# A decoder on one core: in cross-attention, ScalarE's PSUM copy is put ahead of both exponentials of the next step, and its other copies between them

## What is computed

```python
Q = _proj(input_Q, Wq, bq)   # (B, 16, 256, 64)
K = _proj(input_K, Wk, bk)   # (B, 16, 512, 64)
V = _proj(input_V, Wv, bv)
scores = jnp.einsum('bhqd,bhkd->bhqk', Q, K) / np.sqrt(DK).astype(np.float32)
attn = jax.nn.softmax(scores, axis=-1)
context = jnp.einsum('bhqk,bhkd->bhqd', attn, V)
context = context.transpose(0, 2, 1, 3).reshape(input_Q.shape[0], -1, H * DK)
return jnp.einsum('bse,de->bsd', context, Wo)
```

## Time and profile before

| what | value |
|---|---|
| median of 3 runs | 1346.09 us |
| lowest, highest | 1341.35, 1355.59 us |
| the profiled execution | 1355.59 us |
| its span | 1353.9 us |
| its mean granted TensorE clock | 0.952 |
| TensorE matmuls, weight loads | 1207.3, 797.3 us busy |
| VectorE, ScalarE, GpSimd | 736.0, 698.5, 155.3 us busy |

### The profile page before, as it was taken

One profiled execution on the slowest core, in us unless ns is written; L12 is line 12 of the kernel. 1 busy time (PEld: TensorE's weight loads), 2 busy tenths in 40 slices (PEclk: granted clock), 3 DMA queues, 4 the chain that ended last, 5 costly groups with the idle time before them and its releaser, 6 DMA issues.

```text
span 1353.9 us, 21932 instructions
## 1 busy us (share of the span) xinstructions
PE 1207.3 (89%) x7355; PEld 797.3 (59%) x7355; DVE 736.0 (54%) x1882; ACT 698.5 (52%) x1880; POOL 155.3 (11%) x272
## 2 busy tenths in 40 slices
PE   3799989997989998999798999999979999899967
PEld 2573775554766486555486458555557647655546
DVE  5532666676633275667753237566764317566651
ACT  3351675654644186655455238555545507665623
POOL 4310220002020021000211012000022002100000
PEclk9899999999888999999798899999989999999988
DMA  7300000000000000000000000000000000000000
GB/s 226 95 1 0 0 1 1 25 1 1 1 11 1 0 0 1 0 25 1 1 2 9 1 0 1 1 1 25 1 1 9 1 0 0 1 1 1 1 1 8
DMA packets 21060, 15.53 MB, mean 11 GB/s; under 512 B 873, under 2 KB 18647, under 8 KB 20959
## 3 DMA queue, kind: packets, MB, share of 16 engines
q1 hardware_dynamic: 20958, 14.24, 3.6%
HBM read 13.18 MB, written 1.05 MB: 11 GB/s over the span
## 4 chain that ended last, share of the span: by engine, by line
issue 76%; PE 11%; POOL 5%; DVE 3%; POOLq 2%; ACT 1%; SPq 1%; DVEq 0%; DMA 0%; ACTq 0%
PE ps L778 4%; POOL rstd L1415 3%; PE ps L798 2%; PE ps L786 2%; POOLq L1414 1%; PE ps L774 1%; SPq L442 1%; POOL nTok L1454 0%; DVE snm L1774 0%; POOL rms_inv L1415 0%; ACT arena L1225 0%; DVE arena L1769 0%; PE ps L760 0%; POOLq L1437 0%; POOL big L1432 0%
## 5 line engine op out<-in xcount | busy, mean ns | idle before, releaser
L1256 ACT ACTIVATE arena<-ps,nmax 128x512 f32<-128x512 f32 x256 | 176.0, 688 | 200.0 <-PE ps L869 177.1
L1845 DVE TENSOR_REDUCE nmax<-ps 128x1 f32<-128x512 f32 x256 | 164.6, 686 | 107.5 <-PE ps L858 107.5
L1066 ACT ACTIVATE arena<-ps 128x512 f32<-128x512 f32 (+6 forms) x304 | 170.3, 570 | 70.0 <-PE ps L983 13.9
L869 PEld LDWEIGHTS ps<-ident,arena 128*128 128x128 f32 x1024 | 111.0, 142 | 85.3 <-issue 48.1
L869 PE MATMUL ps<-ident,arena 128*128 128x128 f32 x1024 | 147.1, 283 | 4.5 <-ACT arena L1256 4.1
L1850 DVE COPY arena<-ps 128x512 f32<-128x512 f32 x128 | 87.7, 686 | 57.6 <-PE ps L869 57.4
L708 PE MATMUL ps<-big,w1a 128*128 128x512 f32 x256 | 117.3, 604 | 0.0
L1225 ACT ACTIVATE arena<-ps,snm 128x136 f32<-128x136 f32 x256 | 91.8, 375 | 5.8 <-DVE snm L1774 5.8
L1413 POOL TENSOR_TENSOR vare<-mv,eps_ln 128x2 f32<-128x2 f32 x64 | 14.1, 220 | 701.4 <-DVE mv L1526 700.8
L708 PEld LDWEIGHTS ps<-big,w1a 128*128 128x128 f32 x256 | 46.3, 189 | 57.5 <-issue 56.5
L778 PE MATMUL ps<-kT,arena 128*128 128x136 f32 x512 | 77.2, 279 | 0.0
(11 more groups left out here) (348 smaller groups left out, 2190.1 us busy)
## 6 DMA issues: line engine op xcount, KB each, us to landing
ctx<-in_ctx_dram SPq DMA_DIRECT2D x4, 512.0 KB, 4.3
w1a<-in_L_ffn_W_dram SPq DMA_DIRECT2D x1, 2048.0 KB, 10.1
w1b<-in_L_ffn_W_dram SPq DMA_DIRECT2D x1, 2048.0 KB, 11.4
w2b<-in_L_ffn_W_dram SPq DMA_DIRECT2D x8, 256.0 KB, 6.2
X<-in_x_dram SPq DMA_DIRECT2D x4, 256.0 KB, 2.9
out_dram<-Y SPq DMA_DIRECT2D x4, 256.0 KB, 2.3
arena<-in_L_xattn_Wq_dram SPq DMA_DIRECT2D x1, 512.0 KB
arena<-in_L_xattn_Wk_dram SPq DMA_DIRECT2D x1, 512.0 KB
```

The source lines that it names most:

```text
L869: last = pe.transpose(ps[:, 4 + h, k * P:(k + 1) * P], cprob[:, h, k * P:(k + 1) * P], ident[:, :])
L1066: return act.activation(dst, src, ACT.Copy)
L1256: act.activation(cprob[:, h, :], bank(2 * (t % 2) + h), ACT.Exp, bias=nmax[:, s:s + 1], accum_out=rsum[:, j % 2, s:s + 1]).then_inc(c_exp, 1)
L1845: dve.tensor_reduce(nmax[:, s:s + 1], bank(s % 4), AX.X, ALU.max, negate=True)\
```

## The change

ScalarE's `pair(j)` alone changes. The copy of bank 5, which stood between the two exponentials, is put ahead of both, and with it its wait for the second count of `cT_ps` (head 1's transposes), which takes in the wait for the first count that stood ahead of head 0's exponential; that one is gone. `spread`, `queries` and the first `rec_projected`, which stood behind both exponentials, now stand between them.

```diff
                 def pair(j):
                     for t in range(TT):
+                        act.wait_ge(cT_ps, it * (NS * PAIRS) + j * NS + 2 * t + 2)
+                        copy(cprobT[:, 2 * (t % 2) + 1, :], bank(5)).then_inc(cT_odd, 1)
                         nj, nt = (j, t + 1) if t + 1 < TT else (j + 1, 0)
-                        act.wait_ge(cT_ps, it * (NS * PAIRS) + j * NS + 2 * t + 1)
                         if nj < PAIRS:
                             exps(nj, nt, 0)
-                        act.wait_ge(cT_ps, it * (NS * PAIRS) + j * NS + 2 * t + 2)
-                        copy(cprobT[:, 2 * (t % 2) + 1, :], bank(5)).then_inc(cT_odd, 1)
-                        if nj < PAIRS:
-                            exps(nj, nt, 1)
                         if t == 0 and j:
                             spread(j - 1, 7)
                         if t == 1 and j + 1 < PAIRS:
                             queries(j + 1)
                         if t == 2 and j == PAIRS - 2 and more_groups:
                             rec_projected(it + 1, 0, 7)
+                        if nj < PAIRS:
+                            exps(nj, nt, 1)
                         if t == 2 and j == PAIRS - 3 and more_groups:
                             rec_turned(it + 1, 1, 7, R_LNG, R_LNB)
                         if t == 2 and j == PAIRS - 2 and more_groups:
```

## The result

The changed kernel takes 1359.54 us, the median of 5 runs (1354.22 to 1365.11); the kernel before took 1343.81 over 5 runs beside it. The ratio is 1.0122, with a 95% interval from 1.0074 to 1.0171: 15.7 us slower, where 24.4 were forecast.

A forecast was written before the change was run, and what follows sets the result against it. TensorE's queue was taken to set the pace, ScalarE costing only where TensorE waits for it. Terms 17.5 + 4.6 + 1.3 + 1.0 made 24.4 us slower, on the median 1346.1 giving 1370.5; range 1357 to 1386.

The forecast's parts named there:

- step 1: Second step of a head pair, with query and output projections: the projection's earlier start gives back 0.22 us.
- B: The last four of a step's eight TensorE transposes, needing head 1's exponential; taken to start 0.47 us after the first four.
- step 3: Last step of a head pair: value products of 1.95 us outlast ScalarE's lateness, so it loses nothing itself.
- only one delay lands: Rival: the row-sum copy costs the next step's last four transposes nothing; about 12 us slower, 1358 us; chance 0.10.
- A: The first four of a step's eight TensorE transposes, needing head 0's exponential.
- the ordinary pair: Head pair without woven recurrence, first and last pairs excepted: 0.97 us longer on 15.17, 18 times, 17.5 us.
- Step 0: First step of a head pair, with the row-sum copy: the next step's last four transposes come 0.72 us late.
- Step 2: Third step of a head pair, only transposes and scores as cover: head 1's exponential comes late, loss 0.47 us.
- The last group: Fourth group's cross-attention, no recurrence woven in: to end some 8 us later after its start.
- The recurrent pairs: Pairs 5 to 7 of the first three groups: most delay disappears; 0.3 us a group, 1.0 in all.
- The clock fell: Rival: TensorE's stalls drop its clock, 1.5 us a fall, one in each pair, giving 1419 us; chance 0.06.
- The other side: Rival: earlier output projection, exponentials covered, so each of 24 waits shrinks by up to 0.38 us; 1337 us; chance 0.04.

The follow-up runs named there:

- Number 1: Against the kernel before, only the copy of bank 5 put ahead of both exponentials, the small copies left behind them: 1367.2 us, ratio 1.0204.
- number 5: Against the changed kernel, the row-sum copy put back behind both exponentials: 1344.2 us, ratio to the kernel before 1.0008.
- Number 4: Against the kernel before, the wait for head 0's transposes moved from a register instruction onto head 0's exponential: 1342.9 us, ratio 1.0009.
- query and key copy between: Against the kernel before, query copy and the recurrence's key copy put ahead of head 1's exponential, waits as before: 1327.4 us, ratio 0.9892.
- number 2: Against the kernel before, only row-sum, query and key copies put between the exponentials, the copy of bank 5 unmoved: 1336.8 us, ratio 0.9958.
- number 3: Against the kernel before, only the query copy put ahead of head 1's exponential: 1329.2 us, ratio 0.9915.
- number 6: Against the changed kernel, the wait for head 0's transposes kept as well, ahead of the copy of bank 5: 1360.7 us, one run.

## Why the prediction was right, and where it was off

**The direction, the places and the mechanism were right.** TensorE sets the pace, ScalarE's copy ahead of the exponentials makes it wait in step 1 at B and in step 3, and the row-sum copy adds to the first. Number 1 and number 5, whose periods were worked out by the same chain with one constant corrected from the changed kernel's trace, came out at 15.98 and 15.33 as expected. The range of 1357 to 1386 held the time, 2.5 us above its lower end, and that end was set for another mechanism (only one delay lands); the forecast's own range, 1360 to 1384, began just above 1359.5. That the time lies inside is in part luck. Of the signs, the period passed (15.81, over the 15.6 that would have spoken against it) and the hole before L892 went as forecast; the holes came out smaller, 0.43 us in step 1 and 0.37 ahead of step 3 with 0.16 more inside its transposes (1.25 for 1.09), where 0.7 was forecast for each, and the groups 2.3 to 3.4 us longer for 5 to 6, the last 5.5 for 8. The hole in step 1 is smaller than the delay of 0.62 besides, since A's four transposes run for 0.66 us before TensorE is idle: 1.09 from A to B (234.04 to 235.13) less 0.66 is 0.43.

**The term that was too large is the ordinary pair: 0.97 us forecast, 0.64 measured.** By steps:

- Step 0: 0.72 forecast. From A of step 0 to B of step 1 is now 3.61 us (231.52 to 235.13), before 2.99 (2.52 and the 0.47): 0.62.
- Step 1: 0.22 given back by forecast. From B to the projection 2.59 us (235.13 to 237.72) where it was 2.92: 0.33.
- Step 2: 0.47 forecast. B of step 3 has no row of its own. Before, it started 0.59 ahead of the scores behind it (246.30 to 246.89); by the same 0.59 ahead of the scores at 244.39 it starts at 243.80, 3.12 after A of step 2 (240.68), where it was 2.76: 0.36.

Each is 0.10 or 0.11 too high, and each holds the same constant once: the 0.77 to 0.80 from transposes to ScalarE's first instruction. It has three parts.

- 0.08, in all three: I had read the constant from an exponential whose wait stands on a register instruction, and used it for a copy that carries its wait itself. Number 4 shows the 0.08 (register instruction to exponential), and without it both kinds of instruction start 0.69 after the transposes: the copy in the changed kernel (235.13 to 235.82) and the exponential in the last group before (1296.04 to 1296.73). "Nothing is computed anew; what goes is the wait for A alone" priced this at nothing.
- 0.03 to 0.04, in steps 0 and 2: four transposes that begin after a hole take 0.66 us, but eight in a row take 1.09 in all and not 0.47 + 0.66 = 1.13. There the copy starts 0.04 after the end of the eight (1.13 against 1.09), in step 1 0.03 after the end of the four (0.69 against 0.66).
- 0.03, in step 1: the 0.83 read there, taken as 0.80, was not a wait for the transposes. The register instruction starts 0.69 after B there too; the row maximum that the exponential needs is signalled at 237.98, and the exponential starts at 238.01.

**The last group** has the constant of 0.69 before as well. Its period was 15.20 all the same, since in step 1 the exponential waits for its row maximum there too (0.29 us of idle time put to VectorE) and the hole before the output projection is 0.44. It went up by 5.5 us for the 8.3 forecast (6 x 0.97 + 1.15 + 1.3). So "the same in each group" holds for the three looped groups.

**The recurrent pairs:** 0.3 a group was forecast, with bounds from -1 to 9 for the three. Taking pair 0 and four ordinary pairs (0.95 + 2.56) off the group's differences leaves -1.2, -0.1 and -1.2, together -2.5, outside the bounds. The unforeseen part is the clock. The groups that come out 1.2 us ahead, 0 and 2, are those that had no fall of the clock at the end of cross-attention, and group 1, which had one, comes out level. The size fits: between the last normalisation but two and the last but one, kernels that had groups of both kinds show

| kernel | with a fall (mean clock) | without | difference |
|---|---|---|---|
| the change | 19.72 (0.91) | 18.61, 18.61 | 1.11 |
| wait on the exponential | 20.43 (0.92) | 19.16, 19.16 | 1.27 |
| query and key copy between | 19.71 (0.91) | 18.54, 18.53 | 1.17 |

The kernel before has 20.29, 20.30 and 20.26, all with a fall. That the change prevents the fall is not shown: the same program has a fall in one group and none in another, and number 4, with ScalarE's copies and exponentials in the order of before, had one in one group of three. With a fall on both sides the change is 0.58 us faster here (20.30 to 19.72), which is the side of the forecast's lower bound, where the key copy gains its 0.31.

The sum with the measured terms is 18 x 0.64 + 4 x 0.95 = 15.3, and with the last pair and the recurrent ones 13.5 by the stages, against 15.7 with an interval of 10 to 23. Of the 10.9 us between the 24.4 forecast and these 13.5, the constant makes 6.8 (18 x 0.33 and 4 x 0.2), the recurrent pairs 3.5, and the last pair the rest.

**The rivals.** The clock fell nowhere in the ordinary pairs: 1.00 over 100 us with holes of 0.43 and 0.37 us in each 15.81. The rule of the Trainium skill on micro-idles ("TensorE: Matmul & The Clock Gate", "A second HAM failure mode: psum-queue depth-cycling") did not come true here. "Only one delay lands" is out by number 5: the row-sum copy's 0.48 lands in full when the bank copy stands first (in number 2 alone it is 0.3, 15.01 against 14.71). "The other side" is right in its first half, which number 3 took alone, and wrong for the whole change for the reason given, step 2 having no cover.

## What to carry to other kernels

Before moving an instruction in a queue, find for every step what covers the one that is pushed back. Here a 0.6 us copy ahead of an exponential costs 0.5 us in a step whose cover is two score products, and gains 0.45 in the step that ends with the value products; the same edit by step, not for all steps, makes the kernel 1% faster. When a chain is walked with constants, take each from an instruction that gets its wait in the same way: by itself (0.69 us here), behind a semaphore instruction (0.75) or behind a register instruction (0.77). An edit that moves or adds a wait can exchange one of these for another, and the small instructions that the trace holds for the line of the wait show it. And compare stages only where the clock did the same in both.

## What was not expected of the hardware

- A wait that an ACTIVATE does not carry itself costs extra: 0.06 us by a semaphore instruction (numbers 4 and 6), 0.08 by a register instruction (the kernel before). In number 6 it does so although the added wait had long been met.
- TensorE waited 1.82 us for VectorE before and then ran at a clock of 0.50; after the change it waited 1.92 us at the same place of group 0 and stayed at 1.00. The length of one wait did not decide it. A fall costs 1.1 to 1.3 us, and two of them fewer gave the change, slower as a whole, some 2.2 to 2.5 us in the profiled execution.
